# Section 1's scatters at three in two expert units; token preparation of groups 7 and 8 and the logits of section 2 at later units

## The reference

```python
shared = silu(xf @ w1) * (xf @ w3) @ w2                  # 256 -> 512 -> 256
s = sigmoid(concat([xf, tf]) @ router_W)                 # 8 experts
topk_idx = top_k(s + router_bias, 2)                     # two per token
gates = s_sel / (sum(s_sel) + 1e-9)
h = gelu(einsum('nc,ech->enh', xf, W1e)); y = einsum('enh,ehc->enc', h, W2e)
x = x + (shared + sum over the two experts of gate * y) / 3
# then, with z = x, over t = 0..255:
gate = sigmoid(h @ Wh.T + z_t @ Wz.T + b); h = tanh(h * (1 - alpha) + gate * z_t)
x = x + hs
```

## Time and profile before

| | |
|---|---|
| median of 3 runs | 763.66 us (762.21 to 768.95) |
| the profiled execution: its own time | 764.96 us |
| its span (first to last instruction) | 763.1 us |
| PE busy | 700.4 us, 92% |
| DVE, ACT, POOL busy | 547.1, 472.9, 270.8 us |
| chain that ended last | PE 68%, DVE 15%, ACT 8%, DMA 4% |
| mean granted TensorE clock | 0.962 |

### The profile page before, as it was taken

How to read it: one execution, slowest core, us unless ns; L and a number is a source line. 1 busy time by engine, 2 the same in 40 slices (tenths; PEclk the granted TensorE clock), 3 DMA queues, 4 the chain that set the end, 5 groups by cost and what they waited for, 6 DMA issues and landing times.

```text
span 763.1 us, 22288 instructions
## 1 busy us (share of the span) xinstructions
PE 700.4 (92%) x8562; PEld 505.6 (66%) x8562; DVE 547.1 (72%) x2014; ACT 472.9 (62%) x1347; POOL 270.8 (35%) x284
## 2 busy tenths in 40 slices
PE   5899897998999999999999899999999999999763
PEld 3455486645888656898578786566889555686442
DVE  4887651457877698877688786898976678866854
ACT  4746473634677755777676577556877645676533
POOL 2037464265642156452174025773040173002100
PEclk9999998999999999999999999999999999999965
DMA  8836899893896785996869654366475354133101
GB/s 284 326 112 228 220 247 263 204 201 109 208 237 191 166 166 146 216 203 186 208 152 224 112 140 158 127 164 142 105 202 140 113 153 132 43 92 118 43 15 43
DMA packets 166460, 124.73 MB, mean 163 GB/s; under 512 B 118706, under 2 KB 147156, under 8 KB 166356
## 3 DMA queue, kind: packets, MB, share of 16 engines
q1 hardware_dynamic: 150436, 79.19, 44.7%
q0 software_dynamic: 14368, 41.96, 17.3%
q10 hardware_dynamic: 1552, 2.15, 0.8%
HBM read 39.90 MB, written 55.84 MB: 125 GB/s over the span
## 4 chain that ended last, share of the span: by engine, by line
PE 68%; DVE 15%; ACT 8%; DMA 4%; issue 3%; POOL 0%; ACTq 0%; DVEq 0%; POOLq 0%
PE bank L1739 64%; PE bank L1967 2%; DVE hid_low L1507 2%; DVE pre L1561 2%; DMA xe<-x_slots_even 2%; DVE taken L1558 2%; DVE full L1500 1%; PE bank L1902 1%; DMA y_got<-y_slots_even,where 1%; ACT th L1257 1%; ACT hs_high L1265 1%; DVE r_part L1522 1%; DVE r_sum L1526 1%; DVE left L1419 1%; DVE x_parts L1378 1%
## 5 line engine op out<-in xcount | busy, mean ns | idle before, releaser
L1739 PE MATMUL bank<-xe,w1e_high 128*128 128x128 f16 x1360 | 215.9, 221 | 9.5 <-DMA xe<-x_slots_even 5.9
L1739 PE MATMUL bank<-xs,w_high 128*128 128x512 f16 x512 | 167.3, 382 | 5.2 <-DVE w_low L1677 3.0
L1739 PE MATMUL bank<-xe,w1e_low 128*128 128x128 f16 x680 | 146.9, 221 | 1.1
L1739 PEld LDWEIGHTS bank<-xe,w1e_high 128*128 x1360 | 125.5, 99 | 20.9 <-issue 7.8
L1507 DVE TENSOR_TENSOR hid_low<-full,hid_high 128x512 f16<-128x512 f32 (+1 forms) x152 | 102.9, 677 | 49.2 <-ACT hid_high L1210 39.1
L1257 ACT ACTIVATE th<-bank 128x64 f32<-128x64 f32 x256 | 56.9, 222 | 93.3 <-PE bank L1739 89.5
L1265 ACT ACTIVATE hs_high<-pre 128x64 f16<-128x64 f32 x256 | 65.5, 256 | 73.1 <-DVE pre L1561 64.8
L1558 DVE SCALAR_TENSOR_TENSOR taken<-th,zq 128x64 f32<-128x64 f32 x256 | 57.9, 226 | 69.7 <-ACT th L1257 66.8
L1739 PEld LDWEIGHTS bank<-hs_high,gwt_high 128*128 128x128 f16 x1024 | 68.2, 97 | 51.8 <-ACT hs_high L1265 38.0
L1078 POOL TENSOR_TENSOR fence_pool<-zero 128x1 f32<-128x1 f32 x12 | 3.4, 280 | 274.7 <-DMA y_slots_odd<-y_pair 84.7
L1739 PE MATMUL bank<-hs_high,gwt_high 128*128 128x32 f16 x1024 | 79.1, 178 | 20.5 <-ACT hs_high L1265 20.0
(11 more groups left out here) (156 smaller groups left out, 1704.4 us busy)
## 6 DMA issues: line engine op xcount, KB each, us to landing
y_slots_even<-y_pair SPq DMA_DIRECT2D x45, 256.0 KB
y_slots_odd<-y_pair SPq DMA_DIRECT2D x37, 256.0 KB
x_res<-in_x_dram SPq DMA_DIRECT2D x16, 512.0 KB
out_dram<-o_tok SPq DMA_DIRECT2D x32, 256.0 KB, 3.5
x_tok<-in_x_dram SPq DMA_DIRECT2D x14, 512.0 KB
x_slots_even<-zeros POOLq DMA_DIRECT2D x1, 4096.0 KB, 18.1
x_slots_odd<-zeros POOLq DMA_DIRECT2D x1, 4096.0 KB, 15.0
y_got<-in_L_cond_W1e_dram SPq DMA_DIRECT2D x4, 512.0 KB, 13.9
```

Source lines behind the costliest of these rows:

```text
L1739: return pe.matmul(out_ap, w, mov, start=start, stop=stop, skip_group_check=True)
```

## The change

Section 1's 24 scatters (POOL) were spread over units 18 to 29, two for each expert unit. Now they stand at units 17 to 31, three for every two expert units, and the wait function is a new one. The preparation of groups 7 and 8 moves from units 30 and 31 to 32 and 33, and the logits of section 2 from unit 34 to 35; the routing, ranks and placing of section 2 move with them by one unit each.

```diff
-PREP_UNIT = dict(zip(range(N_GROUPS), (-1, -1, 1, 3, 16, 17, 20, 30, 31, 40, 52, 53, 76, 78, 85, 106)))
-LOGITS_UNIT = [2, 9, 34, 56, 90, 111]
+PREP_UNIT = dict(zip(range(N_GROUPS), (-1, -1, 1, 3, 16, 17, 20, 32, 33, 40, 52, 53, 76, 78, 85, 106)))
+LOGITS_UNIT = [2, 9, 35, 56, 90, 111]
 SCATTER_AT = [[_f + _j * _a // _b for _j in range(_n)] for _n, _f, _a, _b in zip(
-    SECTIONS, (7, 18, 39, 63, 96, 118), (1, 1, 1, 1, 2, 1), (2, 1, 1, 1, 3, 1))]
+    SECTIONS, (7, 17, 39, 63, 96, 118), (1, 4, 1, 1, 2, 1), (2, 3, 1, 1, 3, 1))]
...
-            def half(first, i):
-
-                if i % 2 == 0:
-                    pool.wait_ge(s_down, first + i // 2 - DOWN_LAG)
-                else:
-                    pool.wait_ge(s_up, first + i // 2 + 1)
+            def three_in_two(first, i):
+
+                if i % 3 != 1:
+                    pool.wait_ge(s_up, first + 2 * i // 3 + 1)
...
-                        half(SCATTER_AT[1][0], j * TOPK + k)
+                        three_in_two(SCATTER_AT[1][0], j * TOPK + k)
```

## The result

| | before | changed |
|---|---|---|
| median | 763.93 us (759.83 to 768.95, 20 runs) | 768.54 us (763.23 to 773.21, 20 runs) |
| the profiled execution, its span | 764.96, 763.1 us | 767.49, 765.4 us |
| ratio | | 1.0050, 95% interval 1.0032 to 1.0068 |

What follows compares the result with a forecast made beforehand. PE, busy 92%, was taken as the bound, with time to win in its stops and the slow clock behind them. -3.8 (part A) and +1.9 (part B) gave -1.9 us, a median of 761.8 us, range 755.5 to 768.5.

Steps and rivals of the forecast that it cites:

- the landing of group 8's last transpose: Before the logits: 5.0 us from issue at 155.1 with gathers beside it, so landed at 160.1.
- rival 2: Slower: last scatter holds ACT, logits come late; 768.4 us, decided by a transpose landing over 7 us; chance 0.2.
- Part B: Preparations behind the scatters, logits in unit 35: +1.9 us, bounds -1.5 to +7.1.
- part A: Fewer scatters beside the token pairs before unit 26: -3.8 us, bounds 0 and -8.1.
- The clock behind the logits: PE's slow clock of 0.50 following the wait before the logits: as before, 3.4 us.
- wait for y_pair near 142: PE's 0.72 us stop before unit 32's work, behind ACT's two preparations: gone, -0.7 us.
- ACT's wait for the last scatter: ACT, after unit 32's silu, waits 1.6 us in group 7's preparation for the last scatter to land.
- PE's stop behind it: At unit 34, PE waits 1.1 us for unit 33's late silu, a stop absent from the kernel before.
- the low part of unit 38: On DVE, starts 13.7 us behind routing, at 183.7, instead of 182.01.
- The wait of 2 us at unit 39: PE waits about 2 us for unit 39's low part on DVE; its way down starts at 189.4.
- The rule on taking turns: DMA engines alternate between queues by packet; by that alone thinner scatters win only 0.9 us.
- stop A: PE's 4.74 us wait for the token pair before unit 26: shrinks to 2.6, slow clock behind from 6.8 to 3.4 us.

Runs made afterwards that it cites:

- e1_prep_only: Kernel before with preparations of groups 7 and 8 at units 32 and 33 and logits at unit 35, scatters untouched: 769.81 us, ratio 1.0069.
- e5_held_behind: Changed kernel with section 0's gathers held until group 8's last transpose landed and both token loads behind the four transposes: 762.57 us, ratio 0.9985.
- e2_gather_held: Changed kernel with POOL waiting for group 8's last transpose before section 0's first gather: 763.54 us, ratio 0.9985.
- e11: Changed kernel with 12 thin scatters, 12 from the landing of unit 26's pair, gathers held, token loads behind the transposes: 760.47 us, ratio 0.9947.
- e13: The e11 kernel with the load of group 8's tokens also moved to unit 24: 759.30 us, ratio 0.9947 to before.
- e4: Changed kernel with section 2's logits back at unit 34, routing, ranks and placing as before: 770.59 us, ratio 1.0093.
- e6: Changed kernel with scatters two in each unit as before and section 0's gathers held for the last transpose: 764.35 us, ratio 1.0008.
- e8: Kernel before with only section 1's scatters changed: first 15 three in two units, last 9 three in each unit: 766.03 us, ratio 1.0011.
- e9: The e8 kernel with section 2's logits in unit 35: 766.23 us, ratio 1.0038 to before.
- e10: Kernel before with first 12 scatters three in two units, other 12 released by the landing of unit 26's pair: 765.46 us, ratio 1.0015.
- e3: Changed kernel with token loads of groups 9 and 10 issued behind the four transposes of groups 7 and 8: 765.42 us, ratio 1.0011.
- e12: Changed kernel with the load of group 8's tokens moved to unit 24: 765.72 us, ratio 1.0035.

## Why the prediction was wrong

- **The failed step is the landing of group 8's last transpose.** I took 5.0 us "with gathers beside it", next to the 4.41 that I took for quiet; it was 7.88, and 10.05 in e1_prep_only. I had it as rival 2's condition, with 7 us as the deciding point and the 8.50 us of the earlier trace rows as its evidence, and gave that rival 0.2. I put the gathers' start near 150, and two had already gone out by then. Above all, 4.41 was itself not quiet: a token load stood ahead of it, and with neither load nor gathers the landing is 3.2 us (e5_held_behind). No row of before shows that 3.2. What could be read was that gathers come on top of the load; the gathers' own time on the DMA engines was 3.0 us, where I allowed 0.6. 8.50 was the nearer row in size, though it is of another transfer, a pair out of DRAM.
- **How the miss adds up.** Unit 31's way up ends 1.7 us earlier than before in the changed profile, so the forecast's times shift by that. Against them the last transpose goes out 0.5 us late (153.94 against 153.4), lands 2.9 us later than allowed for, and routing starts 10.26 us behind the logits instead of 9.8, since the clock is at 0.50 until 168.0. That is 3.9 us, and 191.65 less the forecast's 189.4, shifted to 187.7, is 3.95. Part B was +1.9 by forecast and +5.85 by the profile, within its bounds of -1.5 to +7.1. With part A's 1.3 us (below) that is 5.2 of the 5.7 us between the forecast (-1.9) and the ratio (+3.8).
- **The clock behind the logits** was put down "as before", 3.4 us; it is 10.2, of which 4.2 us lie ahead of the logits, inside the wait. From the logits to the start of routing it costs 0.5 us more than before.
- **Part A** was over-sized: -3.8 forecast, -2.5 in the profile (E 49.57 to 47.05), -1.7 on the mean. The stop shrank to 2.61 us, where I wrote 2.6, and the slow clock to 3.4, as I wrote. But I charged the 6.8 us of half clock at 3.4 us, where the earlier trace rows show PE busy in 4.92 of them: 2.5 us. The rest of that stretch was the stop itself, counted twice. And one profile's stop was taken for a fixed quantity: with thin scatters it was 2.25 to 4.92 us from one profile to the next. That 2.61 met the forecast 2.6 was luck.
- **Held:** no wait for y_pair near 142; ACT's wait for the last scatter (1.6 us forecast, 1.72 measured) and PE's stop behind it (1.1 and 1.08); the low part of unit 38 13.7 us behind the start of routing (172.22 to 185.97, 13.75) and unit 39's way down 19.4 behind it (19.43). The wait of 2 us at unit 39 came in two pieces: 2.11 us ahead of the sums in front of unit 40's work, for DVE's ranks, and 0.55 us for the low part of unit 39.
- **The rule on taking turns.** The Trainium skill ("DMA: Bandwidth & Descriptors", "Queues, rings and completion order") says that each DMA engine alternates between queues, a packet at a time. In e1_prep_only's 148 to 162 us SP's queue holds 69.0% and POOL's 32.5% of the engines' time:

```profile
q1 hardware_dynamic: 4339, 1.58, 69.0%
q0 software_dynamic: 246, 0.69, 32.5%
```

Stretched by these shares, a landing of 4.4 us (the load, no gathers) would become 4.4 x 101.5 / 69 = 6.5 us; it was 10.05, and 7.88 in the changed kernel. Shares over a fixed window are a poor use of the rule, though: what counts is the work that the gathers put in front of the transpose while it is under way. Over the landing itself POOL's queue held 37.5% of 7.88 us in the changed kernel and 36.9% of 10.05 us in e1_prep_only, 3.0 and 3.7 us of each engine's time. On top of 4.4 us that gives 7.4 and 8.1 us (an estimate from these figures). So the gathers' own time accounts for 3.0 of the 3.5 us of excess in the changed kernel, and for 3.7 of 5.6 us in e1_prep_only. There SP's packets were slower too, 0.050 us each against 0.035 in e2_gather_held (72.5% of 10.05 us on 16 engines in 2340 packets, 112.6% of 4.38 us in 2258); why is open. For stop A, where I had set the rule against my own term, it did better: it allowed a gain of 0.9 us of waiting, I took 2.1, and the means over the profiles are 3.9 us with two scatters a unit and 3.3 with the thin ones.

## What to carry to other kernels

When a change reorders one queue, look up who waits for what stood last in it: here the result's store moved ahead of the transposes, and that released the gathers to run beside them. Price a landing by the most crowded row the trace has, unless you can name what will not run beside it, or add to the quieter row the engine time of what will. Never count the slow clock in time in which the engine is idle. A wait that holds off transfers nobody needs yet (DVE's first read of the gathers' results stands at 176.87 us in the changed kernel, 21 us behind the sixth) can be worth more than an earlier start of urgent ones.

## What the runs showed of the hardware

- The last DMA transpose of group 8 lands in 3.2 to 3.3 us with no load ahead and no gather beside it (e5, e11, e13), 4.2 to 4.8 with a token load ahead and no gather or a single one (before, e2, e4, e6, e8, e9, e10), 5.7 with four gathers and no load (e3), and 7.5 to 10.05 with both (e12, changed, e1). Added to 3.2, the two single effects of 1.2 and 2.5 us would give 6.9.
- During these landings POOL's queue held 1.9 us of each DMA engine's time in e3_loads_behind (33.4% of 5.70 us), 2.6 in e12_load_8_late (34.9% of 7.50), 3.0 in the changed kernel and 3.7 in e1_prep_only: 0.5 to 0.6 us less than the excess over the landing without gathers (3.2 us without the load, 4.4 with it) in the first three, 1.9 us less in the last.
- With PE's waits of 2.25 to 3.01 us between 100 and 200 us came 3.4 us at a granted clock of 0.50 (1.2 GHz), but one of 2.35 us ahead of unit 16 (e8_sparse_then_dense) left it at full speed; with 3.11 to 5.19 us 3.4 or 6.8 us, in no order of their length (4.92 us had 3.4, 3.11 had 6.8); with 6.21 to 8.45 us 10.2 us. The slow stretch often begins inside the wait: before, at 122.2 us in the wait that ended at 124.08. Waits of 0.96 and 1.27 us left the clock at full speed, but 0.84 and 1.65 us were followed by 3.4 us at half clock.
- One execution is a poor measure of a wait for a crowded DMA: E varied by 3.3 us over nine profiles in which the first twelve scatters and the loads were issued by the same rules.
